# State-space layers on one core: C products in pairs, the sum over states by accumulating transposes, the gate token by token, convolution taps read from PSUM

## The reference

```
xz = xn @ W_in ; x_in, z = split(xz)          # xn: layer norm, scaled and shifted; 512 channels each
u  = silu(conv1d(x_in, 4 taps, causal) + b)   # per channel, along the 512 tokens
dt_r, B, C = split(u @ W_x)                   # 64, 16, 16 columns
dt = softplus(dt_r @ W_dt + b_dt)
h[t] = h[t-1] * exp(dt[t] * A) + (dt[t] * u[t]) * B[t]    # 16 states for each of the 512 channels
y[t] = sum over the 16 states of h[t] * C[t]
y = (y + u * D) * silu(z) ;  out = residual + gate * (y @ W_out)
```

## Time and profile before

| | |
|---|---|
| time, median of 3 runs | 3869.78 us (3867.14 to 3873.81) |
| span of the profiled execution | 3873.2 us |
| what lies around the span | at most 0.6 us, if its own time was the longest of the three |
| busy: PE / DVE / ACT / POOL | 2902.1 / 2801.5 / 2089.7 / 1716.0 us |
| mean granted TensorE clock | 0.83 of full |
| layer 1: first instruction to last store | 442.4 to 1611.2 us |
| layer 3: first instruction to last store | 2584.1 to 3864.4 us |

### The profile page before, as it was taken

The page is one execution under the profiler, slowest core; times in us unless marked ns, Lnnn a source line. Parts: engine busy times, 40 slices in busy tenths (PEclk is TensorE's granted clock), DMA queues, the critical chain, the costliest instruction groups (busy, mean ns, idle before and its releaser), DMA issues. The chain is left out here.

```text
span 3873.2 us, 38272 instructions
## 1 busy us (share of the span) xinstructions
PE 2902.1 (75%) x11060; PEld 1488.6 (38%) x11060; DVE 2801.5 (72%) x3410; ACT 2089.7 (54%) x3166; POOL 1716.0 (44%) x1209
## 2 busy tenths in 40 slices
PE   6999667877777877468788878866776866867775
PEld 4555333444444444222333322223434434434443
DVE  1333279999999999755555555515999989999996
ACT  0223267777777777213444444426766756767663
POOL 0000047678677768800000000003767667677686
PEclk7899787988988988768888888768887978878888
DMA  2000111111011101043333333010101011111011
GB/s 78 11 33 22 47 39 44 39 44 50 28 44 50 50 23 55 33 82 63 60 39 66 66 61 61 12 58 33 43 24 60 30 53 50 39 45 61 23 55 49
DMA packets 101857, 176.64 MB, mean 46 GB/s; under 512 B 10219, under 2 KB 88827, under 8 KB 92563
## 3 DMA queue, kind: packets, MB, share of 16 engines
q1 hardware_dynamic: 97430, 161.65, 15.8%
q0 software_dynamic: 4224, 12.59, 1.0%
...
...
## 5 line engine op out<-in xcount | busy, mean ns | idle before, releaser
L965 POOL TENSOR_TENSOR l_h<-l_h,l_c_all 128x512 f32<-128x512 f32 x1024 | 1483.1, 1465 | 709.6 <-DVE l_h L896 688.5
L896 DVE TENSOR_TENSOR_SCAN l_h<-l_dA,l_ps_dbu 128x512 f32<-128x512 f32 x1024 | 1210.1, 1205 | 137.2 <-PE l_ps_dbu L1089 81.8
L1089 PE MATMUL l_ps_dbu<-ident,l_dub 128*128 128x128 f32 x4096 | 691.8, 303 | 282.8 <-DVE l_h L896 256.9
L767 ACT ACTIVATE l_dub<-l_duT,l_b_tok 128x512 f32<-128x512 f32 x1024 | 723.6, 711 | 281.5 <-PE l_ps_dbu L1089 281.5
L1089 PEld LDWEIGHTS l_ps_dbu<-ident,l_dub 128*128 128x128 f32 x4096 | 520.2, 154 | 783.0 <-DVE l_h L896 535.5
L781 ACT ACTIVATE l_dA<-l_dt,l_a_neg 128x512 f32<-128x512 f32 x1024 | 724.1, 711 | 0.2
L1076 PE MATMUL l_ps_y<-l_h,ident 128*128 128x512 f32 x1024 | 630.2, 702 | 104.5 <-DVE l_h L864 103.9
L1346 DVE TENSOR_REDUCE l_q_max<-l_ring 128x2 f32<-128x1024 f32 x256 | 312.7, 1224 | 335.7 <-PE l_ring L1614 332.9
L1499 ACT ACTIVATE l_probs<-l_ring 128x1024 f32<-128x1024 f32 x256 | 261.7, 1024 | 433.3 <-PE l_ring L1623 432.3
L864 DVE TENSOR_TENSOR l_h<-l_h 128x512 f32<-128x512 f32 x512 | 459.8, 901 | 26.1 <-POOL l_h L965 26.0
L925 POOL DMA_INDIRECT l_x_in<-x_dram,l_idx_x x32 | 33.2, 1038 | 951.8 <-DMA l_idx<-in_idx 938.7
...
...
## 6 DMA issues: line engine op xcount, KB each, us to landing
...
l_res<-x_dram SPq DMA_DIRECT2D x24, 512.0 KB, 5.4
...
l_x_in<-x_dram SPq DMA_DIRECT2D x16, 512.0 KB, 5.3
x_dram<-l_res SPq DMA_DIRECT2D x16, 512.0 KB, 3.0
...
```

Of the source, the lines that this page charges most:

```text
L767: return act.activation(dub[:, n % 2, t, :], duT[:, p, t, :], ACT.Copy, scale=b_tok[:, p, t, n:n + 1])
L896: dve.tensor_tensor_scan(h[:, h_slot(s), :], dA[:, s % DA_RING, :], ps_dbu[:, dbu_slot(s), :], 0.0, ALU.mult, ALU.add).then_inc(scan_ok, 1)
L965: pool.tensor_tensor(h[:, h_slot(s), :], h[:, h_slot(s), :], c_all[:, (n // C_GROUP) % 2, n % C_GROUP, :], ALU.mult).then_inc(hc_ok, 1)
L1089: last = pe.transpose(ps_dbu[:, dbu_slot(s), t * P:(t + 1) * P], dub[:, n % 2, t, j * P:(j + 1) * P], ident[:])
```

## The change

- GpSimd multiplies **two units by their C row in one instruction** of 128x1024 (`h` becomes a ring of 16 units). The adds of VectorE are gone.
- TensorE sums over states **for every unit** with four 128x128 transposes that accumulate into `ps_y`, which is now token-major; the skip term is added there by matmuls of `u` with a diagonal of D (`skip`). `SUM_LAG` is 10 units, and at units 10 to 15 the sums wait for the gate of the batch before.
- The input projection's z half comes out token-major (`z_side`); VectorE gates from `ps_y` in four instructions after unit 9 (`silu_gate`); TensorE turns the gated block back (`y_turn`), ScalarE copies it (`y_part`), and then comes the output projection.
- **Taps:** ScalarE makes the last tap with the bias out of `misc` (`conv_part`), and VectorE reads the other three **from `misc`** (`taps`). TensorE may overwrite `misc` with the next x block only after them (`x_side` waits for `cv_ok`).
- `clip`, `dt_max`, `dt_u` and both softplus steps are one 128x2048 instruction each in place of four of 128x512. The gate vector is loaded for each batch.
- All fixed units of the two streams are new. Layer norm statistics of batch b+1 now stand after unit 0, the application after unit 1.

```diff
-DA_RING, DBU_RING = 8, 3
-PAIRED = UNITS // 2
-ADD_LAG, SUM_LAG = 3, 7
+DA_RING, DBU_RING, H_RING = 8, 3, 16
+SUM_LAG = 10
+GATE_AT = SUM_LAG
+SUMS_AT = [[s - SUM_LAG] for s in range(UNITS)]
+SUMS_AT[SUM_LAG:SUM_LAG + 6] = [[], [], [], [0, 1], [2, 3], [4, 5]]
...
                 def c_load(b, p, g):
                     if not (g < 2 and first(b)):
-                        sp.wait_ge(hc_ok, b * UNITS + (g - 1) * C_GROUP * JB + CREDIT)
+                        sp.wait_ge(hc_ok, b * H_PAIRS + (g - 1) * GROUP_PAIRS)
...
+                def conv_part(b, j):
+
+                    act.wait_ge(x_mm, b * JB + j + 1)
+                    if j == 0 and not first(b):
+                        act.wait_ge(dt_ok, b)
+                    c = VEC_LAYOUT[L + "_conv_w"][0] + j * TAPS + TAPS - 1
+                    act.activation(work[:, j, :], misc[:], ACT.Identity, scale=vecs[:, c:c + 1],
+                                   bias=vec(vecs, L + "_conv_b")[:, j:j + 1]).then_inc(tap_ok, 1)
+                def y_part(b, t):
+                    act.wait_ge(y_tr, b * TB + t + 1)
...
+                    act.activation(y[:, t, :], misc[:], ACT.Copy).then_inc(yt_ok, 1)
...
+                def softplus(b):
+                    act.wait_ge(clip_ok, b + 1)
+                    act.activation(work[:], work[:], ACT.Exp).then_inc(dt_exp, 1)
+                    act.wait_ge(dt_exp, b + 1)
+                    act.activation(work[:], work[:], ACT.Ln, bias=1.0).then_inc(ln_ok, 1)
...
-                    if s == 9: ln_rstd(b)
-                    if s in (13, 15): mod(b, (s - 13) // 2)
-                    if s in (17, 19, 21, 23): x_part(b, (s - 17) // 2)
...
+                    if s == 1: ln_rstd(b)
+                    if s in (3, 5): mod(b, (s - 3) // 2)
+                    if s in (7, 10, 13, 16): conv_part(b, (s - 7) // 3)
+                    if s in (26, 28, 30, 32): z_part(b, p, (s - 26) // 2)
+                    if s == 33: silus(b, p)
+                    if s == 37: xd(b, p)
+                    if s == 39: b_copy(b, p)
+                    if s in (41, 43, 45, 47): dt_raw(b, (s - 41) // 2)
+                    if s == 49: softplus(b)
+                    if s in (55, 57, 59, 61): du_tok(b, p, (s - 55) // 2)
...
+                    if s in (18, 20, 22, 24): y_part(b, (s - 18) // 2)
...
+                def taps(b, j):
+
+                    for i in range(TAPS - 1):
+                        k = TAPS - 2 - i
+                        back = TAPS - 1 - k
+                        done = b * JB * (TAPS - 1) + j * (TAPS - 1) + i
+                        if i == 0:
+                            dve.wait_ge(tap_ok, b * JB + j + 1)
+                        else:
+                            dve.wait_ge(cv_ok, done)
+                        c = VEC_LAYOUT[L + "_conv_w"][0] + j * TAPS + k
+                        dve.scalar_tensor_tensor(work[:, j, back:], misc[:, 0:T - back], vecs[:, c:c + 1], work[:, j, back:],
+                                                 ALU.mult, ALU.add).then_inc(cv_ok, 1)
+
+                def silu_gate(b, p, t):
+                    if t == 0:
+                        dve.wait_ge(sum_ok, b * UNITS + UNITS + CREDIT)
+                        dve.wait_ge(u_ok, b * 2 + 2)
+                    dve.tensor_tensor(z[:, p, t, :], ps_y[:, t, :], z[:, p, t, :], ALU.mult).then_inc(yg_ok, 1)
...
-                    if s == 7: ln_stats(b)
-                    if s == 10: ln_apply(b)
-                    if s in (18, 20, 22, 24): conv(b, (s - 18) // 2)
...
+                    if s == 0: ln_stats(b)
+                    if s == 1: ln_apply(b)
+                    if s in (8, 11, 14, 17): taps(b, (s - 8) // 3)
+                    if s == 48: clip(b)
+                    if s == 51: dt_max(b, p)
+                    if s == 52: dt_u(b, p)
...
+                        two = h[:, s % H_RING - 1:s % H_RING + 1, :]
+                        c_row = c_all[:, (n // C_GROUP) % 2, n % C_GROUP:n % C_GROUP + 1, :]
+                        pool.tensor_tensor(two, two, c_row.to_broadcast([P, 2, T]), ALU.mult).then_inc(hc_ok, 1)
...
+                def x_side(b, j):
+                    if j == 0:
                         pe.wait_ge(mod_ok, b * DH + DH)
...
+                        pe.wait_ge(cv_ok, b * JB * (TAPS - 1) + j * (TAPS - 1))
...
+                    for k in range(JB):
+                        last = pe.transpose(misc[:, k * P:(k + 1) * P], z[:, p, t, k * P:(k + 1) * P], ident[:])
+                    last.then_inc(y_tr, 1)
...
+                    if s in (2, 4): xn_half(b, (s - 2) // 2)
+                    if s in (6, 9, 12, 15): x_side(b, (s - 6) // 3)
+                    if s in (25, 27, 29, 31): z_side(b, (s - 25) // 2, after_post)
+                    if s == 36: x_proj(b, p, after_post)
+                    if s == 38: b_turn(b, p)
+                    if s in (40, 42, 44, 46): dt_proj(b, p, (s - 40) // 2)
+                    if s in (54, 56, 58, 60): du_turn(b, (s - 54) // 2, after_post)
...
+                    if s in (17, 19, 21, 23): y_turn(b, p, (s - 17) // 2, has_prep)
+                    if s == 34: out_proj(b, 0, has_prep)
+                    if s == 48: out_proj(b, 1, has_prep)
...
+                    for t in range(TB):
+                        if s == 0 and not first(b):
+                            pe.wait_ge(yg_ok, b * TB - TB + t + 1)
+                        last = pe.matmul(ps_y[:, t, j * P:(j + 1) * P], h[:, s % H_RING, t * P:(t + 1) * P], ident[:],
+                                         start=(s == 0), stop=(s == UNITS - 1), is_transpose=True, skip_group_check=True)
+                    last.then_inc(sum_ok, 1)
...
+                    for t in range(TB):
+                        last = pe.matmul(ps_y[:, t, j * P:(j + 1) * P], u[:, j, t * P:(t + 1) * P], d_diag[:, j, :],
+                                         start=False, stop=False, skip_group_check=True)
```

More of the change, by code:

```diff
@@ L911, in _ @@
             def _(pool):
-                pool.sem_inc(hc_ok, CREDIT)
+                for j in range(JB):
+                    last = pool.tensor_scalar(d_diag[:, j, :], ident[:], vec(vecs, L + "_D")[:, j:j + 1], None, ALU.mult)
+                last.then_inc(fixed_ok, 1)
                 pool.sem_inc(res_ok, CREDIT)
@@ L969, in _ @@
                 batches(pool, body)
-                for j in range(JB):
-                    silu_gate(B - 1, (B - 1) % 2, j)
                 if gathered:
@@ new lines, in sum_states, with skip @@
+                    for t in range(TB):
+                        if s == 0 and not first(b):
[3 more added lines that the diff above has]
+                    last.then_inc(sum_ok, 1)
+                def skip(b, j):
+                    for t in range(TB):
+                        last = pe.matmul(ps_y[:, t, j * P:(j + 1) * P], u[:, j, t * P:(t + 1) * P], d_diag[:, j, :],
+                                         start=False, stop=False, skip_group_check=True)
+                    if j == JB - 1:
+                        last.then_inc(skip_ok, 1)
@@ L1090, in body @@
                         last.then_inc(dbu_ok, 1)
-                        if has_post and s in (47, 49):
-                            out_proj(b - 1, (s - 47) // 2)
+                        if s in (16, 18, 20, 22):
+                            if first(b) and s == 16:
+                                pe.wait_ge(fixed_ok, 1)
+                            skip(b, (s - 16) // 2)
+                        if has_post:
+                            post_step(s, b - 1, 1 - p, has_prep)
                         if has_prep:
@@ L1100, in _ @@
                     sum_states(B - 1, s)
-                for tp in range(OUT_PARTS):
-                    out_proj(B - 1, tp)
+                for s in range(UNITS):
+                    post_step(s, B - 1, (B - 1) % 2, False)
         sems.clear(f"layer{layer}_clear")
```

317 lines of the change are left out of this document (138 added, 179 removed).

## The result

The changed kernel takes **3972.28 us** (median of 4 runs, 3959.41 to 3986.55) against 3871.8 us (median of 4) before: ratio 1.0273, 95% interval 1.0238 to 1.0308, so 100 us slower. The forecast was 3890 with a range to 3985. One of the four executions of all_single, a run further down, took 5686 us at a granted clock of 0.996, which nothing else here resembles; it is left out of that run's median.

A forecast was written before the change was run, and what follows sets the result against it. No engine's floor was above 102 us; waits between engines bound the batch: 144.0 us in layer 1 (+ 4.2), 154.6 in layer 3 (+ 0.5). With openings, batch 7 and tail, + 20 on 3873.8 gave 3894, median 3890 us; range 3775 to 3985.

The forecast's parts named there:

- rival L: Units 18 to 33: low TensorE clock there too, three more low spells, + 5 us a batch, 3950 us; chance 0.14.
- The late x: Layer norm statistics: x queued behind the second C load, VectorE stands some 7.6 us in layer 1, some 18 in layer 3.
- E: The end of the last scan of the batch before, from which the prediction counts times in a layer 1 batch.
- The handoffs: Units 9 to 17: the next projection waits for VectorE's taps, 8.0 us for three units, three times, 24.1 us.
- C: Middle batches: buffers hide the handoffs and ScalarE runs through, 110 us in layer 1, 120 in layer 3; 3480 us; chance 0.12.
- P: Rival theory of the experiments, not the prediction: TensorE's added sums pace the batch; no chance given.
- the clock's 5.2 us: TensorE after idling ahead of four handoffs a batch: each restart at low clock priced 1.3 us, + 5.2 a batch.
- Rival B: Middle batches: same handoffs but no clock loss, 138.8 us in layer 1, 149.4 in layer 3; 3828 us; chance 0.23.
- D: TensorE: transposes alone never bring full clock, about 165 us a batch, 4140 us; chance 0.08.
- the openings: Start of layers 1 and 3: uncovered taps make each block 4.9 us in place of 2.67; + 12 us a layer in all.
- Batch 7: Last batch of each layer: without adds or preparation 79 plus 8 us, - 17 each; the tail after it + 2.5 each.
- Locks: VectorE beside GpSimd: two-operand instructions are stretched, those with one operand in PSUM not; some 5 us a batch of lock waits.

The follow-up runs named there:

- all_single: Changed kernel with early x load, early gather, taps from a copy, TensorE filler and GpSimd products one unit each: 3605.8 us, ratio 0.9337 to the kernel before.
- x_early: Changed kernel with layer 1's x load issued ahead of the second C load: 3931.8 us, ratio 1.0147 to the kernel before.
- gather_early: Changed kernel with layer 3's gather of x moved to GpSimd's 15th pair of the batch before: 3906.7 us, ratio 1.0091 to the kernel before.
- x_copy: Changed kernel with VectorE's taps reading a ScalarE copy, so the next projection waits for ScalarE alone: 3841.2 us, ratio 0.9919 to the kernel before.
- fill: Changed kernel with transposes of a zero tile on TensorE just ahead of places where it idles, batches 1 to 6: 3916.6 us, ratio 1.0127 to the kernel before.
- the lead: Layer norm steps two units later on TensorE and ScalarE: 3726.9 us against 3715.8 on three combined edits, 3593.3 against 3605.8 on all_single.

## Why the prediction came out as it did

The direction was right, and 3972 lies within the range. But it is 82 us above the 3890 of the forecast and above the forecast's own band (3855 to 3930); that the range reached it is owed to rival L.

**What bounds (right).** No engine's floor decides: busy times are 109, 101, 104 and 80 us of 150. The walk through the batch, with the measured ends from the rows above:

| stretch | predicted at full clock | measured |
|---|---|---|
| units 0 to 8 with taps | 27.8 | 30.5 (957.7 to 988.2) |
| units 9 to 17 | 24.1 | 29.5 (to 1017.7) |
| units 18 to 24 | 11.9 | 11.9 (to 1029.6) |
| units 25 to 47 | 43.2 | 46.3 (to 1075.9) |
| units 48 to 63 | 31.9 | 32.5 (to 1108.4) |
| clock | 5.2 | in the rows |
| sum | 144.0 | 150.7 |

**The late x (mechanism right).** In layer 1 the wait was 7.1 us in the batch read against 7.6, but two errors cancel in that: scan 0 ended at E + 2.9 in place of E + 1.1, and x was there at E + 10.0 in place of E + 8.7 (issued at 961.14, used at 967.70: 6.6 us, where 5.3 was the median landing). The statistics to the end of the application then took 6.4 us in place of 5.3, so the batch was 2.5 us late at E + 16.5, before TensorE had restarted. In layer 3 x was there at E + 16.8 (3029.6 to 3046.4) in place of E + 19.3, and the waits were 13.5 in the mean against 18; this is most of why layer 3's batch missed its forecast by 2.9 us and layer 1's by 6.0. x_early and gather_early show that the wait is a cause: 6.1 and 10.2 us a batch.

**The handoffs (mechanism right).** x_copy shows it. C falls: ScalarE is busy 104 of 150 us, not throughout. P falls to fill.

**The size that was short in the batch: the clock's 5.2 us.** From the rows and their neighbours, against the same groups at full clock, the spells at 1.2 GHz cost TensorE 2.0 us at 974.27 (five groups by 0.85 in place of 0.44), 1.6 at 988.27, 2.4 at 997.48, 1.6 at 1007.95, 1.7 at 1053.54, 1.1 behind the softplus and 2.0 at 1093.88: 12.4 us in seven spells, not 5.2 in four. At the handoffs the 5.2 was nearly right: the three x projections cost 5.6, and the turned block behind the last taps nothing (0.66 us at 1017.76, after 3.52 us idle; the windows there show 1.00, so the length of a stop alone does not decide). What the sum had at nothing were the other four spells, 6.8 us. Not all of this is on the path. The three handoffs took 9.2, 10.5 and 9.8 us, together 5.4 more than the 24.1, about the 5.6 of their spells; the x projection's 1.7 lies in a stretch that was 3.1 late. The 2.0 at 974.27 hardly shows (scan 8 ended 11.9 us after the application, 11.6 were forecast), and the 3.1 in the last stretch at most with its 0.6. So the 6.7 us by which the batch read missed 144.0 are by this walk 2.5 of x and layer norm, some 2 of clock beyond the 5.2, and some 2 that are not taken apart. In fill, with part of the spells gone, the batch was 4.6 us shorter, so the clock is on the path with at least that.

Rival L (3950) came nearest and had three more low spells at + 5 a batch; four more came, 6.8 us, but not where it put them: in units 18 to 33 (1018 to 1046) the windows show 1.00. Rival B (no clock loss) falls to fill, and D to the 1.00 windows.

**The size that was short in the openings.** "Each block is 2.0 + 0.6 + 2.3 = 4.9" took a projection at full clock. It runs at 1.2 GHz behind each wait there:

```profile
444.03 3.78 PE L995 MATMUL l_misc<-l_modT,l_w_in 128*128 128x512 f32 x4 [3.22 <-DVE l_work L858]
```

and blocks came every 7.00 us in layer 1 (444.03, 451.03, 458.03) and every 6.82 in layer 3 (taps at 2669.12, 2675.94, 2682.77, 2689.59). Openings with batch 0 cost 48 in place of 21. Up to the x projection the two layers lost 19.0 and 12.4 us in place of 7.5 each, 16.4 more, and four blocks each at 2.1 and 1.9 us over 4.9 are 16.1: that is the clock. The other 10 us came behind the x projection, mostly in layer 1's batch 0; x_copy took back 5.6 of them there, and no run takes the rest apart.

**Batch 7** was right in the sum, -28.7 against -29, and partly by luck: -11.4 in layer 1 and -17.3 in layer 3. In sum, of the 82 us by which the layers were short, 55 are middle batches and 27 the openings; some 40 of the 82 can be put down to the clock (2 us in twelve batches and the 16 of the openings, taking layer 3's batches to be as layer 1's, an estimate).

**Locks (half right).** I kept 5 us a batch for locks; that pairs lengthen three steps by 1 us each I missed. It was inside the 31.9 of the last stretch (32.5) and the 3.26 of the layer norm (3.39), so it made no error in the sum, but it is most of the 46 us that the change gave away.

Open: some 2 us of a middle batch and 10 us of the openings, the part of gather_early's missing 3 us that is no lock, and what the lead is worth.
